# Summing message slots with accumulated float32 transposes in PSUM

## The reference

```
w_m = (efeat @ W_msg  + b_msg ).reshape(E, 16, 16)      # [edge, in i, out o]
w_a = (efeat @ W_attn + b_attn).reshape(E, 16, 16)
h   = feat[src][:, :, None]
e1, e2 = w_m * h, w_a * h
ex   = exp(e2 - segment_max(e2, dst)[dst])
attn = ex / segment_sum(ex, dst)[dst]
ft   = segment_sum(e1 * attn, dst).sum(axis=1)          # sum over i
x = layernorm(x + ft); x = layernorm(x + mean of the edge features of each node)
```

## Time and profile before

| | |
|---|---|
| median of 3 runs | 2993.66 us (2983.25 to 3000.31) |
| the profiled execution: span | 2950.2 us |
| its own time beside the span | not recorded apart; the median of the runs is 43.5 us above the span |
| TensorE busy (matmul records) | 2137.9 us, 72% |
| DVE, POOL, ACT busy | 1862.0 (63%), 1687.5 (57%), 1256.9 us (43%) |

### The profile page before, as it was taken

One profiled execution on the slowest core, in us unless ns is written; L12 is line 12 of the kernel. 1 busy time (PEld: TensorE's weight loads), 2 busy tenths in 40 slices (PEclk: granted clock), 3 DMA queues, 4 the chain that ended last, 5 costly groups with the idle time before them and its releaser, 6 DMA issues. The chain is left out here.

```text
span 2950.2 us, 21765 instructions
## 1 busy us (share of the span) xinstructions
PE 2137.9 (72%) x6682; PEld 952.6 (32%) x6682; DVE 1862.0 (63%) x2907; ACT 1256.9 (43%) x1228; POOL 1687.5 (57%) x1845
## 2 busy tenths in 40 slices
PE   2347676676877777877787658877787767887777
PEld 1213233232333333333333223333333323333333
DVE  6246465566666666666676547766667656786776
ACT  3223443434444443454454325444444444554444
POOL 6556355665655565555565465655656565655633
PEclk8658888897988888989888889988989888988988
DMA  6000000000000000000000000000000001001000
GB/s 229 16 10 11 8 12 10 10 10 9 10 9 9 14 10 9 10 14 10 10 13 9 9 10 13 10 12 9 10 12 9 12 9 28 12 8 16 8 2 3
DMA packets 60073, 47.60 MB, mean 16 GB/s; under 512 B 28366, under 2 KB 55439, under 8 KB 59436
## 3 DMA queue, kind: packets, MB, share of 16 engines
q0 software_dynamic: 57632, 29.73, 8.0%
q1 hardware_dynamic: 2316, 16.38, 1.5%
HBM read 44.00 MB, written 1.90 MB: 16 GB/s over the span
## 5 line engine op out<-in xcount | busy, mean ns | idle before, releaser
L652 POOL DMA_INDIRECT AR<-in_xt,AR x1607 | 1538.8, 958 | 974.1 <-DVE AR L1472 491.3
L1128 PE MATMUL PX<-AR,CS 128*128 128x512 f32 x3246 | 1663.7, 642 | 37.8 <-issue 23.9
L1472 DVE CUSTOM_DVE_ANT_1 AR<-PW,AR 128x1024 f32<-128x1024 f32 x815 | 979.6, 1221 | 896.8 <-remote 651.2
L1108 PE MATMUL PW<-WS,LT 100*128 100x512 bf16 x1630 | 549.1, 423 | 683.9 <-DVE AR L1472 511.8
L1128 PEld LDWEIGHTS PX<-AR,CS 128*128 128x128 f32 x3246 | 664.9, 206 | 652.1 <-issue 532.4
L888 ACT ACTIVATE LT<-PTB 100x1024 bf16<-100x1024 bf16 (+1 forms) x221 | 211.2, 956 | 1005.7 <-remote 601.0
L1485 DVE TENSOR_TENSOR AR<-AR,PX 128x1024 f32<-128x1024 f32 (+1 forms) x442 | 501.0, 1134 | 121.3 <-ACT PX L944 76.0
L1108 PEld LDWEIGHTS PW<-WS,LT 100*128 100x128 bf16 x1630 | 141.5, 103 | 1113.7 <-DVE AR L1472 543.2
L946 ACT ACTIVATE AR<-AR 128x2048 f32<-128x2048 f32 (+1 forms) x221 | 412.9, 1869 | 7.2
L950 ACT ACTIVATE PX<-AR 128x1024 f32<-128x1024 f32 (+1 forms) x221 | 212.4, 961 | 412.3 <-DVE AR L1485 294.8
L944 ACT ACTIVATE PX<-AR 128x1024 f32<-128x1024 f32 (+1 forms) x221 | 231.0, 1045 | 39.4 <-DVE AR L1485 30.1
(11 more groups left out here) (192 smaller groups left out, 517.7 us busy)
## 6 DMA issues: line engine op xcount, KB each, us to landing
AR<-in_xt,AR POOLq DMA_INDIRECT x1607
AR<-in_eat SPq DMA_DIRECT2D x3, 3128.0 KB
AR<-in_eat SPq DMA_DIRECT2D x1, 3120.0 KB
y_d<-AR SPq DMA_DIRECT2D x1, 784.0 KB
AR<-y_d SPq DMA_DIRECT2D x1, 784.0 KB
AR<-in_es,E0I POOLq DMA_INDIRECT x48
y_d<-AR POOLq DMA_INDIRECT x36
CS<-in_cst SPq DMA_DIRECT2D x1, 442.0 KB, 5.3
```

Source lines behind the costliest of these rows:

```text
L652: g.indirect_dma_start(feat(h, j - j0, j - j0 + 1), None, xt, bass.IndirectOffsetOnAxis(ap=node, axis=0)).then_inc(hg_sem(h), 16)
L1108: i = pe.matmul(PAIRS[s % 2][:, j, :], LT[:, g % 3, lo:lo + 128], WS[:, :], start=True, stop=True)
L1128: i = pe.matmul(PDR, IDN, x, start=(a == 0 and j == 0), stop=(g == LAST[k] and j == n - 1))
L1472: v.tensor_tensor_reduce(em(g, j, j + 2).rearrange("p (x c) -> p x c", c=32), w, hb, 1.0, LOW, ALU.mult, ALU.max, accum_out=MXC[:, k % 2, ...
```

## The change

- The slot sum: for each slot four float32 transposes of 128x128 take the place of the product with the identity. The stationary operand is now the slot's data (128 nodes by 128 channels, every second float32 in memory), the moving one is the identity (128 columns). Blocks 0 and 1 are the weights' channels, 2 and 3 the products'. PDR therefore holds [128 channels, 4 blocks of 128 nodes].
- The layout in EMR goes from (i, a, o) to (i, o, a), where a is attention or message: the weights of the product W and the constants are reordered, and every access to one half (`kind`) steps by two elements, where it took runs of 16.
- `weigh` keeps the reciprocal and the product (L1504, L1505) and loses the sum over i (L1506). In its place TensorE makes two small float32 products for each chunk (`channels`): stationary the 128 channels by 128 nodes of a half of TPT, moving a constant of 128x16 (SEL). Their result FT2 lies in the first 16 float32 columns of PTB.
- New order and waits: TensorE's `channels(k)` stands at the start of the step in which `result(k)` was (for the last two chunks at the end of the step before), and waits for DVE's `weigh(k)` and until ACT has copied all transposes made so far out of PTB (`TAKEN`). ACT's `result(k)` moves from the end of the step to its start and waits for `channels`. The next T waits for that `result` (`LENT`). DVE's product in `weigh(k)` waits for `channels(k - 1)`.

The diff, without the parts that only reorder the other path, rename or enlarge the constants:

```diff
+TAKEN, LENT, made = {}, {}, 2
+for i in range(NST):
+    if FINS.get(i - 4, NC) < NC - 2:
+        TAKEN[FINS[i - 4]] = made
+        if made < NGR:
+            LENT[made] = FINS[i - 4]
+    made += i < len(STEPS) and STEPS[i][0] is not None and STEPS[i][0] + 2 < NGR
+TAKEN[NC - 2] = TAKEN[NC - 1] = NGR
...
+        SEL = CS[:, 884:900]
...
-        FT2 = reg([128, 2, 16])
...
+        FT2 = PTB[:, 0:32].bitcast(f32)
...
+        def kind(g, a, lo=0, hi=None):
+            return em(g, lo, hi).rearrange("p (r a) -> p a r", a=2)[:, a, :]
...
                 def result(k):
-                    a.wait_ge(S["v_fin"], k + 1)
-                    a.activation(OUTR[:, k, 0:16], FT2[:, k % 2, :], ACT.Copy, scale=POS[:, k:k + 1]).then_inc(S["a_out"], 1)
+                    a.wait_ge(S["p_ft"], k + 1)
+                    a.activation(OUTR[:, k, 0:16], FT2, ACT.Copy, scale=POS[:, k:k + 1]).then_inc(S["a_out"], 1)
...
                         sums(FINS[i - 2])
+                    if FINS.get(i - 4, NC) < NC - 2:
+                        result(FINS[i - 4])
                     if c is not None:
-                        x, w, shift = weights(c)
+                        both, x, e, shift = weights(c)
...
-                        a.activation(half(w), x[:, 0:w, :], ACT.Exp, bias=shift).then_inc(S["a_x"], 1)
+                        a.activation(e, x[0], ACT.Exp, bias=shift).then_inc(S["a_x"], 1)
                         a.wait_ge(S["a_x"], 2 * c + 1)
-                        a.activation(x, x, ACT.Exp, bias=shift).then_inc(S["a_exp"], 1)
+                        a.activation(both, both, ACT.Exp, bias=shift).then_inc(S["a_exp"], 1)
...
-                        a.activation(half(w), x[:, w:2 * w, :], ACT.Copy).then_inc(S["a_x"], 1)
+                        a.activation(e, x[1], ACT.Copy).then_inc(S["a_x"], 1)
                     if p is not None and p + 2 < NGR:
                         evac(p + 2)
-                    if FINS.get(i - 4, NC) < NC - 2:
-                        result(FINS[i - 4])
...
                     if g >= 1:
                         pe.wait_ge(S["a_T"], g)
+                    if LENT.get(g) is not None:
+                        pe.wait_ge(S["a_out"], LENT[g] + 1)
...
-                        x = em(g, j, j + 1).rearrange("p (i a o) -> p a i o", a=2, o=16)
-                        i = pe.matmul(PDR, IDN, x, start=(a == 0 and j == 0),
-                                      stop=(g == LAST[k] and j == n - 1))
+                        for b in range(4):
+                            x = kind(g, b // 2, j, j + 1)[:, 128 * (b % 2):128 * (b % 2) + 128]
+                            i = pe.matmul(PDR[:, 128 * b:128 * b + 128], x, IDN, is_transpose=True,
+                                          start=(a == 0 and j == 0 and b == 0), stop=(g == LAST[k] and j == n - 1),
+                                          skip_group_check=True)
...
+                def channels(k):
+                    pe.wait_ge(S["v_wt"], k + 1)
+                    if k == NC - 1:
+                        pe.wait_ge(S["v_jn"], 1)
+                    pe.wait_ge(S["a_T"], TAKEN[k])
+                    for h in range(2):
+                        i = pe.matmul(FT2, TPT[:, 128 * h:128 * h + 128], SEL, start=(h == 0), stop=(h == 1))
+                    i.then_inc(S["p_ft"], 1)
...
+                    if FINS.get(i - 4, NC) < NC - 2:
+                        channels(FINS[i - 4])
                     for x in range(4):
                         if x < len(ahead):
                             W(*ahead[x])
...
+                    if FINS.get(i - 3, 0) >= NC - 2:
+                        channels(FINS[i - 3])
...
                 def gm(g, h):
-                    w = 8 * GRP[g][2]
                     v.wait_ge(S["a_x"], 2 * g + 1 + h)
-                    y = em(g).rearrange("p (x a o) -> p x a o", a=2, o=16)[:, w * h:w * h + w, 1, :]
-                    v.tensor_tensor(y, y, EXP[:, 0:16 * w].rearrange("p (x o) -> p x o", o=16), ALU.mult).then_inc(S["v_gm"], 1)
+                    n = GRP[g][2]
+                    y = kind(g, 1, n * h // 2, n * (h + 1) // 2)
+                    v.tensor_tensor(y, y, EXP[:, 0:128 * n], ALU.mult).then_inc(S["v_gm"], 1)
...
-                    if k >= 2:
-                        v.wait_ge(S["a_out"], k - 1)
-                    d = DNR
-                    link(v.reciprocal(RRT, d[:, 0:256]))
-                    link(v.tensor_tensor(TPT, d[:, 256:512], RRT, ALU.mult))
-                    v.tensor_reduce(FT2[:, k % 2, :], TPT.rearrange("p (i o) -> p o i", o=16), AX.X, ALU.add).then_inc(S["v_fin"], 1)
+                    link(v.reciprocal(RRT, DNR[:, 0:256]))
+                    if k >= 1:
+                        v.wait_ge(S["p_ft"], k)
+                    v.tensor_tensor(TPT, DNR[:, 256:512], RRT, ALU.mult).then_inc(S["v_wt"], 1)
```

More of the change, by code:

```diff
@@ L238, in gnn_kernel @@
         E0I = sb("E0I", [128, NC], i32)
-        CS = sb("CS", [128, 884])
+        CS = sb("CS", [128, 900])
         IDN, TRI, E127 = CS[:, 0:128], CS[:, 128:256], CS[:, 256:257]
@@ L399, in gnn_kernel @@
         S = {n: sem(n) for n in names}
+        for here, there in (("v_wt", "v_fin"), ("p_ft", "p_fx"), ("v_jn", "v_rmax")):
+            S[here] = S[there]
         d_xi = [sem(f"d_xi{i}") for i in range(2)]
@@ L618, in _ @@
             g.wait_ge(S["g_m"], 1)
-            flv = FLW[:, :].rearrange("p (i a o) -> p i a o", a=2, o=16)
+            flv = FLW[:, :].rearrange("p (i o a) -> p i a o", a=2, o=16)
             g.memset(flv[:, :, 0, :], PADS).then_inc(S["g_m"], 1)
@@ L892, in sums @@
                     if k >= 1:
-                        a.wait_ge(S["v_fin"], k)
+                        a.wait_ge(S["v_wt"], k)
                     a.activation(DNR, PDR, ACT.Copy).then_inc(S["a_dn"], 1)
                 def result(k):
-                    a.wait_ge(S["v_fin"], k + 1)
-                    a.activation(OUTR[:, k, 0:16], FT2[:, k % 2, :], ACT.Copy, scale=POS[:, k:k + 1]).then_inc(S["a_out"], 1)
+                    a.wait_ge(S["p_ft"], k + 1)
+                    a.activation(OUTR[:, k, 0:16], FT2, ACT.Copy, scale=POS[:, k:k + 1]).then_inc(S["a_out"], 1)
                 def weights(g):
                     k, j0, n, x = GRP[g]
-                    return em(g).rearrange("p (x a o) -> p x a o", a=2, o=16)[:, :, 0, :], 8 * n, CM[:, 1, k:k + 1]
-                def half(w):
-                    return EXP[:, 0:16 * w].rearrange("p (x o) -> p x o", o=16)
+                    return kind(g, 0), [kind(g, 0, n * h // 2, n * (h + 1) // 2) for h in range(2)], EXP[:, 0:128 * n], CM[:, 1, k:k + 1]
                 def first(k):
@@ L1009, in weights @@
                          .then_inc(S["a_mc"], 1)
-                        v = EM[:, t % 3, :].rearrange("p (x a o) -> p x a o", a=2, o=16)[:, :, 0, :]
+                        v = EM[:, t % 3, :].rearrange("p (x o a) -> p x a o", a=2, o=16)[:, :, 0, :]
                         a.wait_ge(S["v_sub"], 2 * t + 2)
@@ L1563, in joined @@
                         link(v.tensor_tensor(means, means, wide(RCL[:, REST - 2:REST]), ALU.mult))
-                    v.wait_ge(S["v_fin"], k + 1)
-                    link(v.scalar_tensor_tensor(YS[:, k - MAIN, :], FT2[:, k % 2, :], POS[:, k:k + 1], YS[:, k - MAIN, :],
-                                                ALU.mult, ALU.add))
+                    v.wait_ge(S["p_ft"], k + 1)
+                    v.scalar_tensor_tensor(YS[:, k - MAIN, :], FT2, POS[:, k:k + 1], YS[:, k - MAIN, :],
+                                           ALU.mult, ALU.add).then_inc(S["v_jn"], 1)
+                    v.wait_ge(S["v_jn"], k - NC + 3)
                 def centre(lo, hi):
@@ L1838, in scans @@
                         v.wait_ge(S["a_exp"], t)
-                        x = EM[:, (t - 1) % 3, :].rearrange("p (x a o) -> p x a o", a=2, o=16)
+                        x = EM[:, (t - 1) % 3, :].rearrange("p (x o a) -> p x a o", a=2, o=16)
                         for h in range(2):
@@ L1954 @@
                            np.full((NBT - 1) * EB - E - FAKE, 1 << 20, dst.dtype)])
-    wa, wm = (np.asarray(inputs[f"L0_gnn_W_{k}"]).reshape(16, 16, 1, 16) for k in ("attn", "msg"))
-    ba, bm = (np.asarray(inputs[f"L0_gnn_b_{k}"]).reshape(1, 16, 1, 16) for k in ("attn", "msg"))
-    wc = np.concatenate([np.concatenate([wa, wm], 2), np.concatenate([ba, bm], 2)], 0).reshape(17, 512)
-    cst = np.zeros((128, 884), np.float32)
+    wa, wm = (np.asarray(inputs[f"L0_gnn_W_{k}"]).reshape(16, 16, 16, 1) for k in ("attn", "msg"))
+    ba, bm = (np.asarray(inputs[f"L0_gnn_b_{k}"]).reshape(1, 16, 16, 1) for k in ("attn", "msg"))
+    wc = np.concatenate([np.concatenate([wa, wm], 3), np.concatenate([ba, bm], 3)], 0).reshape(17, 512)
+    cst = np.zeros((128, 900), np.float32)
     p = np.arange(128)
@@ L1970 @@
     cst[:, 868:868 + CAND] = CAND - np.arange(CAND)
+    cst[:, 884:900] = p[:, None] % 16 == np.arange(16)
     c = np.arange(50)
```

6 lines of the change are left out of this document (3 added, 3 removed).

## The result

The changed kernel takes 3147.55 us (median of 4 runs, 3142.38 to 3156.15), the kernel before 2988.45 us beside it (4 runs, 2970.35 to 3000.31). The ratio is 1.054, interval 1.0486 to 1.0594: 159 us slower, where I forecast 2590 us. It lies above the top of my range. The profiled execution of the changed kernel took 3142.38 us with a span of 3140.6, so 1.8 us lie around the span. The two profiled executions are 190 us apart (3140.6 against 2950.2), more than the medians, because the one before was a quick one; losses read by comparing the two traces are therefore some 30 us too large over the span.

What follows compares the result with a forecast made beforehand. TensorE's side, chiefly its slot sum, was taken as the bound; from 2993.7 us, 371 off the middle stage, 17 off the end chain and 20 off the first 300 us gave 2590 us, range 2380 to 2970 us.

Steps and rivals of the forecast that it cites:

- Reading the bound: Middle stage, 1.715 us for a slot: TensorE's side, with its slot sum as largest part, is what others wait for.
- The step that failed: DVE's idle time before its products, 0.61 us for a slot, scaled with the slot sum to 0.31 us.
- The price of a transpose: Slot sum as four float32 transposes, paced by their weight loads: 0.11 us each, 0.44 us for a slot.
- The clock: TensorE's mean granted clock, 0.88 in the middle stage, expected near 0.75, so TensorE needs 0.95 us for a slot.
- L1506 and `channels`: Dropping L1506 saves DVE 25.1 us in the stage; new waits and DVE and POOL catching each other allowed 87 us.
- The layout: Stepping by two float32 at L944, L946, L950 and L1485 was taken to cost nothing.
- The end: Chain of 78 slot-sum records at the end, 34.0 us, was to fall by half: 17 us less.
- The slower rival: Float32 transposes pay all passes and their loads aren't hidden: TensorE needs 1.89 us for a slot, 3280 us; chance 0.15.
- its point of 1.44: Time in us of a slot's four transposes with loads beyond which TensorE passes 1.715 us and the kernel gets slower.
- The sign I named: "Remote" waits before DVE's product and ACT's copy fall by about half; staying near 580 and 500 us means the second rival.
- the second rival: TensorE's semaphore lateness may be unrelated to the slot sum: DVE's 0.61 us for a slot stay, 2950 us; chance 0.21.

Runs made afterwards that it cites:

- run 2: Changed kernel with two of each slot's four float32 transposes, so half of the sums left out: 2914.79 us, ratio 0.975 to the kernel before.
- run 9: Kernel before with each product with the identity issued as two products of 256 columns, same work: 3191.76 us, ratio 1.069.
- run 1: Kernel before with every bf16 transpose issued three times to the same place: 3279.19 us, ratio 1.096.
- run 6: Changed kernel with all gathers kept, each for 64 rows instead of 128: 3210.0 us, ratio 1.071 to the kernel before.
- run 7: Kernel before with DVE adding the second half of each slot group onto the first, TensorE summing half the slots: 2791.3 us, ratio 0.933.

## Why the prediction was wrong

- **Reading the bound.** I had each engine's need, saw that all lie below 1.715 us, and saw in the earlier trace rows that TensorE's semaphores come 10 us after its records. Then I read that as "TensorE's side, with its slot sum as the largest part (1523.3 of 1898.8 us), is what the others wait for". The first half was right, the second was not: run 2 took 0.62 of the 0.86 us of each slot away and brought 67 us in all, L1506 included.
- **The step that failed:** "I scale that with the slot sum, 0.44 / 0.86: 0.31 us". The idle time of DVE did not fall from 0.61 to 0.31 us for a slot, it rose to (2600 - 1528.7) / 1410 = 0.76. What it grows with is the count of TensorE's instructions while POOL streams: the kernel loses 33 ns for each in run 9, 46 in run 1 with the transposes' own work in it, against roughly 0.05 us for each us of work. With these the change comes out: 6884 more instructions by 33 ns are 227 us, 0.38 us less work in 1630 slots by 0.05 are -31, L1506 -29: +167, measured +159. That is a fit to these runs at this pace of gathers, not a price to carry away.
- **The price of a transpose** was right: 0.44 us for a slot forecast, 0.48 measured at the full clock. The Trainium skill (TensorE: Matmul & The Clock Gate, Terms) gives a factor of four, by which it would be 0.215 us for a slot; the rows show 0.86 / 0.48 = 1.8, each transpose here having its own float32 weight load.
- **The clock**: mean near 0.75 forecast, 0.73 measured. The rule of the Trainium skill (TensorE: Matmul & The Clock Gate, Part 4: PE-mode transpose) that transposes don't count for it would have held the clock low throughout, and that was not so: in the short stretch shown above, 1504 to 1509.6 us, the granted clock was 1.00 (2.4 GHz), with 24 float32 and 6 bf16 transposes among TensorE's 38 matmuls. Eight products lie between them, so this is no clean test of the rule.
- **L1506 and `channels`.** DVE's work fell as forecast. `channels` and the jostling of DVE and POOL were allowed 87 us; leaving `channels` out gave about 30.
- **The layout.** L1515 kept its 1219 ns (1217 before). ACT's exponentials did not: L961 takes 2218 ns where L946 took 2002, and over the span ACT is busy for 77 us more, which I took at nothing. ACT is at 42%, so I don't count it as a cause, but no run tested it alone.
- **The end** of the chain I took 17 us off. From the last gather to the end it takes 143 us (2997.6 to 3140.6), where it took 149 (2800.9 to 2950.2): 6 us less.
- **The rivals.** The second named the mechanism, "with the stream of gathers, or with the number of instructions, which grows from 8 to 12 for a slot", and then priced it as if the lateness would stay as it was: 2950. A mechanism that depends on a count which the change raises by half must be priced as growing; by that it would have been the slower case. The slower rival that I did price (transposes as costly as four products) had the sign but not the mechanism: TensorE needs 0.48 + 0.215 + 0.057 = 0.75 us, far below its point of 1.44 for the transposes alone.
- **The sign I named** pointed the right way: the waits for "remote" would fall by half, and "if they stay near 580 and 500 us, the second rival holds". They rose to 784 and 669 us.

What stays open: which part of the chip delays TensorE's semaphores, and whether it is also TensorE's own issue that is held up; why half rows made it slower (run 6); how much of run 7 comes from fewer instructions and how much from POOL's slower stream; whether it is POOL's instructions or the packets of its own queue; and whether matmuls or weight loads count. Each time here comes with a span and a granted clock, so its execution was recorded; that an unrecorded one loses the same is not shown.

## What to carry to other kernels

Where waits before an engine's consumers are put down to "remote" while its records show it done, as here, suspect that its work is not the bound and that taking work off it buys little: find what runs beside those waits and price the change by what that depends on, here the count of TensorE's instructions. Beside a dense stream of gathers issued by POOL, few wide TensorE instructions were better here than many small ones, even at more work, and so was letting another engine with room halve their number. A change that is right for its engine can be worth 6% or cost 5% according to what streams next to it, so test it once with the stream thinned out.

## What the runs showed of the hardware that was not expected

- TensorE's semaphores reached ACT and DVE 9 to 16 us after the ends of its records in the place shown, after POOL had begun to issue gathers every 1.25 us; single waits for them before DVE's products lasted up to 25.7 us. Of DVE's 99 longer waits for them 57 ended 1 to 4 us after POOL had paused. The wait fell from 897 to 68 us when half of the gathers were left out, and to 5% of the stage where SP issued them as plain DMAs with twice as many packets in all.
- At the same work, 6492 more TensorE instructions cost 211 us beside that stream (run 9).
- A gather's time on POOL hardly depends on its rows: 959 ns for 128, 914 for 64. Beside DVE's float32 additions of 2048 elements the mean rose to 1114 ns, one gather in eight taking 1.5 to 3 us.
- A float32 transpose with its weight load goes every 0.119 us at the full clock.
- ACT's exponential over 2048 float32 took 2218 ns in the new layout, 2002 in the old.
